# First expert matrices kept in SBUF and copied into a ring of three by VectorE, with the opening work list of GpSimd reordered

## The reference

```
x = x + xattn(layernorm(x), ctx)            # 16 heads of 8 features, softmax over 128 keys
xf = layernorm(x).reshape(4096, 128)
top_vals, top_idx = top_k(xf @ router_w.T, 2)
probs = softmax(top_vals)
for e in range(8):
    w = sum(where(top_idx == e, probs, 0))
    h = gelu(xf @ w1[e].T + b1[e])          # w1[e]: 512 x 128 -> 512 hidden
    y = h @ w2[e].T + b2[e]                 # back to 128
    out = out + w * y
x = x + out
```

## Time and profile before

| what | before |
|---|---|
| median of three executions | 394.74 us (393.62 to 395.11) |
| the profiled execution | 396.63 us, its span 394.9 us |
| mean granted TensorE clock | 0.956 of full speed |
| busy: PE, PEld, DVE, ACT, POOL | 325.1, 260.3, 253.1, 231.7, 231.8 us |
| moved by DMA | 59.94 MB, of it w1 71 times 256 KB |
| attention phase, tile phase, end | 0 to 218, 218 to 381, 381 to 394.9 us |

### The profile page before, as it was taken

How to read it: one execution, slowest core, us unless ns; L and a number is a source line. 1 busy time by engine, 2 the same in 40 slices (tenths; PEclk the granted TensorE clock), 3 DMA queues, 4 the chain that set the end, 5 groups by cost and what they waited for, 6 DMA issues and landing times.

```text
span 394.9 us, 11551 instructions
## 1 busy us (share of the span) xinstructions
PE 325.1 (82%) x3721; PEld 260.3 (66%) x3721; DVE 253.1 (64%) x751; ACT 231.7 (59%) x567; POOL 231.8 (59%) x384
## 2 busy tenths in 40 slices
PE   2659699999979898978787976969899999999950
PEld 1226466666656665656555865968789999999840
DVE  4855779999868778769943623645554555446762
ACT  2313569798868768667766423545456666566530
POOL 8745252724758567563667487565766656565550
PEclk9999989999999899999996888999999999999995
DMA  4664463555535424411143563666547767659946
GB/s 131 179 176 114 111 187 96 99 129 161 146 100 142 123 76 120 126 46 45 32 118 99 171 188 108 180 204 185 170 123 254 216 207 213 179 184 317 295 137 186
DMA packets 60618, 59.94 MB, mean 152 GB/s; under 512 B 13797, under 2 KB 45188, under 8 KB 60560
## 3 DMA queue, kind: packets, MB, share of 16 engines
q1 hardware_dynamic: 53504, 46.61, 42.6%
q0 software_dynamic: 4320, 8.47, 6.2%
q10 hardware_dynamic: 2736, 4.13, 3.3%
HBM read 34.90 MB, written 11.63 MB: 118 GB/s over the span
## 4 chain that ended last, share of the span: by engine, by line
PE 65%; DVE 13%; issue 9%; ACT 6%; DMA 3%; POOL 1%; another core or an unknown queue 1%; SPq 0%; DVEq 0%; POOLq 0%; ACTq 0%
PE sexp L1196 16%; PE smax L1184 16%; PE smax L1062 7%; PE tail L1106 7%; DVE shift L1351 4%; PE feed L1053 2%; PE feed L1038 2%; ACT probs L871 2%; PE prep L1130 2%; PE sexp L1070 2%; PE heads L1122 2%; PE feed L1048 2%; PE prep L1137 1%; DMA stacks<-result_d 1%
## 5 line engine op out<-in xcount | busy, mean ns | idle before, releaser
L1351 DVE TENSOR_REDUCE shift<-smax 128x4 f32<-128x512 f32 x128 | 87.0, 682 | 35.1 <-PE smax L1062 34.0
L1184 PE MATMUL smax<-probs,w_ring 128*128 128x128 f32 x568 | 79.2, 284 | 14.3 <-issue 12.8
L793 POOL DMA_INDIRECT result_d<-y_out,stacks x71 | 70.8, 997 | 30.5 <-issue 28.8
L1184 PEld LDWEIGHTS smax<-probs,w_ring 128*128 128x128 f32 x568 | 71.2, 197 | 17.7 <-issue 17.2
L871 ACT ACTIVATE probs<-sexp 128x512 f32<-128x512 f32 x128 | 74.4, 595 | 12.9 <-PE sexp L1070 11.6
L704 POOL DMA_INDIRECT dispatch_d<-rows_out,row_i x64 | 63.0, 984 | 30.6 <-issue 14.8
L1196 PE MATMUL sexp<-w_sb,probs 128*128 x568 | 78.6, 282 | 2.0 <-ACT probs L1005 1.2
L1826 DVE TENSOR_TENSOR probs<-smax,b_cols 128x512 f32<-128x512 f32 x71 | 49.0, 691 | 44.3 <-issue 15.9
L1196 PEld LDWEIGHTS sexp<-w_sb,probs 128*128 128x128 f32 x568 | 70.5, 195 | 5.8 <-issue 5.6
L1005 ACT ACTIVATE probs<-probs 128x512 f32<-128x512 f32 x71 | 44.8, 631 | 37.3 <-DVE probs L1826 27.3
L1062 PE MATMUL smax<-stacks 64*128 64x128 bf16 x512 | 51.3, 230 | 17.2 <-DVE shift L1351 9.7
(11 more groups left out here) (221 smaller groups left out, 502.6 us busy)
## 6 DMA issues: line engine op xcount, KB each, us to landing
w_ring<-w_t_dram SPq DMA_DIRECT2D x71, 256.0 KB
stacks<-kpart SPq DMA_DIRECT2D x46, 128.0 KB
stacks<-qpart SPq DMA_DIRECT2D x46, 128.0 KB
stacks<-dispatch_d SPq DMA_DIRECT2D x71, 65.0 KB
stacks<-result_d ACTq DMA_DIRECT2D x12, 256.0 KB
xw<-x_dram SPq DMA_DIRECT2D x8, 256.0 KB, 3.3
w_sb<-w_t_dram SPq DMA_DIRECT2D x8, 256.0 KB
out_dram<-xw SPq DMA_DIRECT2D x8, 256.0 KB
```

Source lines behind the costliest of these rows:

```text
L793: nc.gpsimd.indirect_dma_start(out=result_d, out_offset=bass.IndirectOffsetOnAxis(ap=xg[r][:, D + 1:D + 2].bitcast(U32), axis=0), in_=y_ou ...
L1184: last = nc.tensor.matmul(up_ps[i][:, c * P:(c + 1) * P], w1_ring[t % WRING][:, c * P:(c + 1) * P], xg_t[i], start=True, stop=True)
L1351: nc.vector.tensor_reduce(shift4[n % 2][:, hp, 0, 4 * m:4 * m + 4], smax[hp][:], AX.X, ALU.max, negate=True).then_inc(max_taken, 1)
```

## The change: what it does

1. A new buffer `w1_sb` holds all eight w1 matrices. SyncE loads one of them at each of the steps 2, 6, ..., 30 of the attention phase.
2. `load_w1` is gone from SyncE's list, with its waits and the register reads of experts. In the start-up, SyncE now waits, for tiles 2 to 11, for the load of the tile two before.
3. The ring `w1_ring` has three buffers in place of six, and VectorE fills it: `copy_w1(t)` copies w1_sb[e] to the ring buffer t % 3, two tiles ahead, behind `sum_y(t-1)`. It waits for `up_done` of the tile three before. The copies for tiles 0 and 1, and the first read of the experts, stand at step 34 of the attention phase.
4. TensorE's `up(t)` waits for the copy (`w1_copied`) in place of the load.
5. GpSimd's opening list is reordered, and the third part of group 1's queries (`split_low(1, qrest, ...)`) moves from its end to step 1, behind the first `split_shift`.

```diff
-WRING = 6
+WRING = 3
...
+        w1_sb = sb("w1_sb", [P, EXPERTS, FF])
...
+                if s % GB == 2:
+                    e = s // GB
+                    sp.dma_start(w1_sb[:, e:e + 1], w1_t[:, e:e + 1]).then_inc(w1_loaded, 16)
                 if s and s % GB == 0:
...
-            def load_w1(t, r, e):
-
-                if t >= WRING:
-                    sp.wait_ge(up_done, t - WRING + 1)
-                sp.dma_start(w1_ring[r][:], w1_t.rearrange("p e f -> p (e f)")[:, bass.ds(e * FF, FF)]).then_inc(w1_loaded[r], 16)
...
-            for t in range(AHEAD):
-                load_w1(t, t, experts[t])
...
-                if 0 < t < WRING:
-                    sp.wait_ge(xg_loaded[t - 1], 16)
-                if t >= AHEAD:
-                    load_w1(t, t % WRING, experts[in_bulk(t)])
+                if 2 <= t < TRING:
+                    sp.wait_ge(xg_loaded[t - 2], 16)
                 load_tile(t, t % TRING, starts[in_bulk(t)])
...
-            split_low(1, qrest, qpart, q_split)
...
                 if s == 1:
+                    split_low(1, qrest, qpart, q_split)
                     set_keys(2)
...
-                pe.wait_ge(w1_loaded[t % WRING], 16 * (t // WRING + 1))
+                pe.wait_ge(w1_copied, t + 1)
...
+            def copy_w1(t):
+
+                if t == 0:
+                    dve.wait_ge(w1_loaded, 16 * EXPERTS)
+                if t >= WRING:
+                    dve.wait_ge(up_done, t - WRING + 1)
+                nc.vector.tensor_copy(w1_ring[t % WRING][:], w1_sb[:].rearrange("p e f -> p (e f)")[:, bass.ds(experts[t] * FF, FF)]).then_inc(
+                    w1_copied, 1)
...
+                if s == LAST_SLOT - 2:
+                    read_experts(0)
+                    for t in range(AHEAD):
+                        copy_w1(t)
...
             for t in range(TILES):
...
+                add_bias(t, t % 2, experts[t])
                 if t:
+                    sum_y(t - 1, (t - 1) % 2, experts[t - 1])
+                if t + AHEAD < TILES:
+                    if bulk_at(t + AHEAD):
+                        read_experts(t + AHEAD)
+                    copy_w1(t + AHEAD)
                 between(t)
```

More of the change, by code:

```diff
@@ L328, in xattn_ffn @@
         xg_loaded = [sem(f"xg_loaded{i}") for i in range(TRING)]
-        w1_loaded = [sem(f"w1_loaded{i}") for i in range(WRING)]
+        w1_loaded = sem("w1_loaded")
+        w1_copied = sem("w1_copied")
         xg_turned = sem("xg_turned")
@@ L521, in _ @@
             sp.wait_ge(table_steps, FIRST_STEPS)
-            experts = table_values(mybir.EngineType.SP, expert_of, 0, EXPERTS - 1)
             starts = table_values(mybir.EngineType.SP, start_of, 0, EXPERTS * REGION)
-            for t in range(AHEAD):
-                load_w1(t, t, experts[t])
             sp.wait_ge(sexp_done, UNITS * OLD_BATCHES)
@@ L543, in _ @@
                 if t and bulk_at(t):
-                    experts = table_values(mybir.EngineType.SP, expert_of, t, EXPERTS - 1)
                     starts = table_values(mybir.EngineType.SP, start_of, t, EXPERTS * REGION)
-                if 0 < t < WRING:
-                    sp.wait_ge(xg_loaded[t - 1], 16)
-                if t >= AHEAD:
-                    load_w1(t, t % WRING, experts[in_bulk(t)])
+                if 2 <= t < TRING:
+                    sp.wait_ge(xg_loaded[t - 2], 16)
                 load_tile(t, t % TRING, starts[in_bulk(t)])
@@ L637, in _ @@
             query_scale(0)
+            clear_queries(1)
+            split_low(0, krest, kpart, k_split)
             set_keys(1)
-            split_low(0, krest, kpart, k_split)
-            clear_queries(1)
+            prepare_values(0)
             query_scale(1)
             scale_rows(1)
-            prepare_values(0)
             split_low(1, krest, kpart, k_split)
             query_scale(2)
-            split_low(1, qrest, qpart, q_split)
             def constants():
@@ L1589, in stat_row, with read_experts @@
                     row_stats(GB * s + u, GB * s + u + 1)
+            experts = {}
+            def read_experts(t):
+                experts.update(enumerate(table_values(mybir.EngineType.DVE, expert_of, t, EXPERTS - 1), t))
+            def copy_w1(t):
[5 more added lines that the diff above has]
+                    w1_copied, 1)
             for s in range(LAST_SLOT + 1):
@@ L1835, in _ @@
             dve.wait_ge(bias_loaded, 32)
-            experts = table_values(mybir.EngineType.DVE, expert_of, 0, EXPERTS - 1)
             for t in range(TILES):
-                before_e = experts[in_bulk(t - 1)] if t else None
-                if t and bulk_at(t):
-                    experts = table_values(mybir.EngineType.DVE, expert_of, t, EXPERTS - 1)
-                add_bias(t, t % 2, experts[in_bulk(t)])
+                add_bias(t, t % 2, experts[t])
                 if t:
-                    sum_y(t - 1, (t - 1) % 2, before_e)
+                    sum_y(t - 1, (t - 1) % 2, experts[t - 1])
[3 more added lines that the diff above has]
+                    copy_w1(t + AHEAD)
                 between(t)
@@ L1847, in _ @@
                     add_found(g)
-            sum_y(TILES - 1, (TILES - 1) % 2, experts[in_bulk(TILES - 1)])
+            sum_y(TILES - 1, (TILES - 1) % 2, experts[TILES - 1])
             for g in range(FIRST_GROUPS - 1, GROUPS):
```

## The result

The changed kernel takes 399.94 us where before takes 396.49 (medians of 20 runs each, all of one comparison): ratio 1.0086, 95% interval 1.0058 to 1.0114. So it is between equal and 0.9% slower, and not 2.5% faster as forecast; both comparisons exclude that. The profiled execution took 402.97 us, with a span of 401.2.

The account below looks back on a forecast made before the run. TensorE sets the pace from tile 32; stalls from full queue plus row sends cost 21.4 us before. Terms -11.5 + 1.7 + 2 - 2 = -9.8 us, 386.8 profiled, 385 us median; range 378 to 395.5.

Parts of the forecast that it names:

- The first term, -11.5 us: Tiles 1 to 31: without the w1 loads the queue stalls go, tile 32 transposed at 288.5 instead of 300.06.
- What ends the first stall is a drained DMA queue: TensorE's stall at 230.70: it resumes as DMA engines fall from 0.80 to 0.16 busy, after six w1 loads.
- I read the stalls as needing both: First-half TensorE stalls: claimed to need a full DMA queue and GpSimd's row sends together.
- the rival that follows from it: Row sends own the first-half stalls; half of the 11.5 us stay lost, 391 us; chance 0.17.
- nothing is lost in the second: From tile 32 up to the add_found tiles, TensorE alone sets the pace, 1.90 us a tile.
- The floors worked out for GpSimd and VectorE: Next limits for tiles 1 to 31: tile 32 at about 285 by GpSimd, about 286.5 by VectorE.
- The copy, 0.5 us: VectorE's w1 copy, taken between 0.34 and 0.69 us; free in undisturbed tiles, in idle time ahead of add_bias.
- The estimate scaled from the tier table: Copy on VectorE: 0.43 us, scaled from the skill's 1.227 us for 2048 fp32 elements.
- The add_found tiles, +1.7 us: Tiles 62 to 70: VectorE has no room, so four copies cost 0.42 us each; bounds 0 and +2.8.
- The attention loads, +2 us: Eight added w1 loads in the attention phase, stalls possible at steps 14, 18, 22; bounds 0 and +8.
- The opening, -2 us: GpSimd's opening: earlier shift split lets TensorE's transpose come at about 27.1 instead of 29.38; bounds -2.5 and +0.5.
- The copy as a lock on GpSimd: Rival: copies stretch GpSimd's indirect DMAs by their length, last send 12 us later, 393.5 us; chance 0.12.

Follow-up runs that it names:

- both comparisons: The changed kernel against the kernel before, measured twice, the second time on another chip: ratios 1.0086 and 1.0002.
- With the read moved away: Changed kernel with table reads one tile earlier, behind copy and add_found, and the first two copies at steps 35 and 36: 0.9953 of before.
- paired sends: Kernel before with the new opening, its last eight row sends in four pairs at tiles 9, 13, 17, 21: 397.99 us, one execution.
- The eight spare sends: Kernel before with eight more GpSimd row sends at tiles 36, 39, ... 57, rows of 520 or 512 bytes: 407.83 and 408.18 us.

## Why the prediction was wrong

**The first term, -11.5 us, failed, at the step "What ends the first stall is a drained DMA queue".** The queue did drain at 232, but TensorE stalls just the same with a queue at 0.25. Tiles 1 to 32 take 82.9 to 85.0 us in the five executions with copies, 84.2 without copies or loads, and 81.1 to 88.9 in the seven with loads: the term is 0, within the scatter of the first half. "I read the stalls as needing both" put the sends in as a condition and the loads as the cause; the sends among the stores are enough. The evidence against it was at hand and told in the prediction: the second half has a DMA share of 0.71 and TensorE busy 61.47 us of 62. I gave the rival that follows from it 0.17. Nor did I line up the gaps with GpSimd's rows: in the profile of before, every gap over 0.6 us between tiles 2 and 31 begins within 3 us behind a send's start, and five of the eight end 3.4 to 3.6 us behind it. And "nothing is lost in the second" half was not quite so: the three stores at 340.74 cost about 1 us of tile 53 there, without a send. The floors worked out for GpSimd and VectorE were never reached and decided nothing. Nor is the rival's own 391 us right, which let half of the term go.

**The copy, 0.5 us, was right in size** (0.418), **and its cost in the undisturbed tiles was small but not nothing.** Tiles 32 to 62 take 59.4 to 60.3 us with copies and 58.7 to 59.1 with loads, 0.8 more. It is at every eighth tile, where the table read now stands with the copy: tiles 31 to 33 take 6.2 us in the changed kernel and 5.9 before, and tiles 39 to 41 and 47 to 49 as well. With the read moved away they take 5.9 again. The other undisturbed tiles still take 1.90. The estimate scaled from the tier table of "VectorE: DVE Perf Modes" in the Trainium skill was 0.43 us; the trace, with 0.418, agrees.

**The add_found tiles, +1.7 us, were undersized as a term, though the copies themselves cost less than that:** 16.9 to 17.0 us with loads and 18.8 to 20.4 with copies, 2.6 more on average. What I had left out is the table read at tile 62, in the same place as an `add_found`: without copies but with the read it takes 17.9 us, 0.9 more than before, and the copies bring it to 18.8, another 1.0. With the read moved away, copies and all take 17.5. The rest, 1.6 us in two of four executions, is the lower clock behind the wait in tile 64. These parts are single executions. The end behind tile 70 is 0.6 us longer as well (17.6 against 17.0), which I had not foreseen; without the copies it is 17.1.

**The attention loads, +2 us: 0** (1.0004). Their price came from a stall laid on a load. The added loads cost nothing. That stall also stands behind two sends 1.3 us apart, which I hadn't looked at; a run without its w2 load was not made.

**The opening, -2 us, was right and somewhat too small:** 2.7 us at the first `attn_t`, and 0.7 to 1.0% at the end, 2.9 to 4.0 us of 400. At tile 1 it is 1.6 us on average, from 221.0 to 219.4, over the profiled executions other than that with paired sends.

**The copy as a lock on GpSimd.** The rule that the Trainium skill gives in "SBUF — State Buffer", on SBUF's two separate sides, would have had an indirect DMA wait for a whole copy, 12 us over the first half. The stores are 31 ns longer on average and the sends 3 (987 against 984). So the two do hold each other up, but not for their whole length: a store that had begun 0.52 us ahead of a copy took 1055 ns, 63 more than the 992 of an undisturbed one. The price is 2.2 us of stores and 1.8 of copies over 71 tiles. In "Who interferes with whom" the same page of the Trainium skill says that a DMA never contends with a compute engine. The eight spare sends cost TensorE 1.3 us each; by what path they do it is open, so the runs don't refute the sentence, but whoever plans by it misses the largest loss of this phase.

The sum by what was measured: 0 for the stalls, -2.9 to -4.0 for the opening, 0 for the loads, and 0.8 + 2.6 + 0.6 = +4.0 for the copies, with the table reads and the clock in it. That is 0 to +1.1 us, 0 to 0.3% slower, between the two comparisons (1.0002 and 1.0086). The step-34 copies may cost more; single profiles don't resolve it, since with the same opening the attention phase varies by about 2 us between executions, and by 6 with that of the paired sends. Why the two comparisons of the same kernels lie 0.8% apart is open.

## What to carry to other kernels

Before a stall is laid on one of two things that coincide, look for the stretch that has only one of them; and where none has, put the suspect into the clean stretch and count the gaps, as eight spare sends did here in one run. A stall with "issue" or a late signal behind it should be lined up with every engine's DMA starts and the distance between them, not only with the busiest queue. Here that suggests keeping a row send 1.5 us or more from the stores on both sides, which no run tried. Work that is moved from a queue to an engine with idle time is free only in tiles in which nothing else stands at that place: list the tiles with a table read, an addition of results, or both, and price those.

## What the hardware showed

An indirect DMA that GpSimd issues between two stores, 128 rows of 512 or 520 bytes, costs TensorE 1.3 us, with matmuls that touch none of its data, and in the cases shown 3.4 us pass from its start to TensorE's resumption. An operation of GpSimd of the same length costs 0.24 us (58.6 less 56.7 us, over eight). Stores alone do the same where they start 1.4 us apart: TensorE's signal is then 1.2 us behind its recorded end instead of 0.15 (tile 53 of before). A copy of 128x512 fp32 within SBUF takes 0.418 us on VectorE; one that starts 0.55 us or more into an indirect DMA of GpSimd ends up to 0.25 us behind its end, after up to 0.695.
